# The causal mask of an attention moved from TensorE's product into VectorE's row maximum

## What is computed

```
H, DH, RAMP, NEG = 16, 64, 32, -1000000000.0
q, k, v = heads of query @ Wq, query @ Wk, query @ Wv        # 8 x 16 heads x 1024 x 64
w = jnp.einsum('bhqd,bhkd->bhqk', q, k) / DH
causal = jnp.triu(jnp.full((s, s), NEG, dtype=w.dtype), k=1)
w = jax.nn.softmax(w + causal, axis=-1)
mask = jnp.clip((arange(s) + span_val * s) / (RAMP + 1), 0.0, 1.0)   # per head, per key
w = w * mask
w = w / (jnp.sum(w, axis=-1, keepdims=True) + 1e-08)
out = (w @ v, heads side by side) @ Wo
```

## Time and profile before

| | |
|---|---|
| runs | median 3530.09 us of 3 (3526.44 to 3532.24) |
| profiled execution | span 3527.3 us; no separate time beside it, so the median lies 2.8 us above this span |
| TensorE busy in the span | 3383.0 us (96%) |
| VectorE | 2916.8 us (83%) |
| ScalarE | 2350.8 us (67%) |
| GpSimd | 848.4 us (24%) |
| mask products L1360 | 1024, from 581.4 to 3009.1 us |
| row maxima L1542 | 1024, 766.1 us busy |

### The profile page before, as it was taken

How to read it: one execution, slowest core, us unless ns; L and a number is a source line. 1 busy time by engine, 2 the same in 40 slices (tenths; PEclk the granted TensorE clock), 3 DMA queues, 4 the chain that set the end, 5 groups by cost and what they waited for, 6 DMA issues and landing times.

```text
span 3527.3 us, 77883 instructions
## 1 busy us (share of the span) xinstructions
PE 3383.0 (96%) x29872; PEld 3071.4 (87%) x29872; DVE 2916.8 (83%) x4672; ACT 2350.8 (67%) x4307; POOL 848.4 (24%) x911
## 2 busy tenths in 40 slices
PE   4999996999999999999999999999999999799998
PEld 4999995888888888888888888888888888699998
DVE  8999974888888888888888878878887888899996
ACT  4666543677777777777767777777777777465664
POOL 3443321221222122122122122212122212233332
PEclk9999997999999999999999999999999999899999
DMA  3332204345445455455445445545534545111111
GB/s 123 95 123 87 93 33 124 97 117 125 125 109 126 109 142 125 112 125 122 109 126 137 116 109 134 125 103 141 134 98 107 145 104 153 54 49 55 55 54 37
DMA packets 160338, 375.19 MB, mean 106 GB/s; under 512 B 19824, under 2 KB 62832, under 8 KB 159728
## 3 DMA queue, kind: packets, MB, share of 16 engines
q1 hardware_dynamic: 159984, 370.37, 40.0%
HBM read 129.38 MB, written 39.58 MB: 48 GB/s over the span
## 4 chain that ended last, share of the span: by engine, by line
PE 64%; DVE 10%; issue 6%; ACT 2%; POOL 2%; POOLq 0%; ACTq 0%; DVEq 0%
PE at_t_ps L1370 11%; PE at_side_ps L1285 9%; PE at_o_ps L1386 8%; PE ffn_gu_ps L505 7%; PE at_s_ps L1356 6%; PE at_s_ps L1357 6%; PE at_side_ps L1297 5%; PE at_side_ps L1334 4%; PE ffn_down_ps L530 4%; DVE at_neg_max L1542 3%; DVE at_eT_lo L1548 3%; PE at_s_ps L1360 1%; PE ffn_hT_ps L475 1%; PE at_side_ps L1324 1%; DVE at_oT_lo L1510 1%
## 5 line engine op out<-in xcount | busy, mean ns | idle before, releaser
L1548 DVE SCALAR_TENSOR_TENSOR at_eT_lo<-at_t_ps,at_eT_hi 128x512 f16<-128x512 f32 (+3 forms) x1536 | 852.2, 555 | 328.8 <-ACT at_eT_hi L1462 322.9
L1462 ACT ACTIVATE at_eT_hi<-at_t_ps 128x512 f16<-128x512 f32 (+3 forms) x1536 | 756.7, 493 | 333.3 <-PE at_t_ps L1370 322.6
L1455 ACT ACTIVATE at_e_rows<-at_s_ps,at_neg_max 128x1024 f32<-128x1024 f32 (+7 forms) x1024 | 759.7, 742 | 152.2 <-DVE at_neg_max L1542 144.7
L1370 PE MATMUL at_t_ps<-at_ident,at_e_rows 128*128 128x128 f32 x4608 | 798.8, 284 | 0.0
L1542 DVE TENSOR_REDUCE at_neg_max<-at_s_ps 128x1 f32<-128x1024 f32 (+7 forms) x1024 | 766.1, 748 | 19.4 <-PE at_s_ps L1360 15.6
L1386 PE MATMUL at_o_ps<-at_v_cols,at_eT_hi 128*128 128x132 f16 x4608 | 611.5, 222 | 2.1 <-DVE at_eT_lo L1548 1.6
L1356 PE MATMUL at_s_ps<-at_kh_st,at_q_st 128*128 128x512 f32 (+2 forms) x1536 | 583.0, 380 | 19.0 <-issue 9.1
L1386 PE MATMUL at_o_ps<-at_v_cols,at_eT_lo 128*128 128x66 f16 x4608 | 567.2, 192 | 0.0
L1357 PE MATMUL at_s_ps<-at_kl_st,at_q_st 128*128 128x512 f32 (+2 forms) x1536 | 514.1, 342 | 0.0
L1370 PEld LDWEIGHTS at_t_ps<-at_ident,at_e_rows 128*128 128x128 f32 x4608 | 491.7, 141 | 0.1
L1386 PEld LDWEIGHTS at_o_ps<-at_v_cols,at_eT_hi 128*128 128x128 f16 x4608 | 432.5, 98 | 25.7 <-issue 18.8
(11 more groups left out here) (211 smaller groups left out, 7088.3 us busy)
## 6 DMA issues: line engine op xcount, KB each, us to landing
at_kh_st<-at_k_hi SPq DMA_DIRECT2D x256, 256.0 KB, 4.5
at_kl_st<-at_k_lo SPq DMA_DIRECT2D x256, 256.0 KB, 5.9
at_w_qk<-w_qk_split SPq DMA_DIRECT2D x65, 512.0 KB, 7.4
at_q_st<-at_q_hi SPq DMA_DIRECT2D x128, 256.0 KB, 3.8
at_q_st<-at_q_lo SPq DMA_DIRECT2D x128, 256.0 KB, 4.8
at_w_v<-w_v_split SPq DMA_DIRECT2D x66, 256.0 KB, 6.0
at_w_out<-w_out_split SPq DMA_DIRECT2D x32, 512.0 KB, 3.7
ffn_x_rows<-in_L_attn_query_dram SPq DMA_DIRECT2D x32, 256.0 KB, 3.2
```

The costliest lines, as they stand in the source:

```text
L1370: last = nc.tensor.transpose(t_ps[i % TBUF][:, b * P:(b + 1) * P], e_rows[:, n % 4, (k0 + b) * P:(k0 + b + 1) * P], ident[:])
L1455: nc.scalar.activation(e_rows[:, n % 4, :w], s_ps[n % 2][:, col:col + w], ACT.Exp, bias=neg_max[:, n % 4:n % 4 + 1]).then_inc(sem("exp_don ...
L1462: nc.scalar.activation(eT[0][:, i % EBUF, :count * P], t_ps[i % TBUF][:, :count * P], ACT.Copy, scale=PSCALE).then_inc(sem("eT_hi"), 1)
L1548: nc.vector.scalar_tensor_tensor(out=eT[1][:, i % EBUF, :count * P], in0=t_ps[i % TBUF][:, :count * P], scalar=PSCALE, in1=eT[0][:, i % EB ...
```

## The change

The mask product is left out. `strip` is a row of 1024 numbers per partition in SBUF: zeros, and in its last 128 columns the triangle with +1e9 above the diagonal. Queries are now scaled by -1/64 rather than 1/64, so the score buffer holds negated scores. `row_max` becomes a fused VectorE instruction that reads the negated scores from PSUM and the last w columns of the strip from SBUF, writes their sum into `e_rows` in SBUF, and reduces it to a minimum. The exponential then runs from `e_rows` to `e_rows`, with scale -1. The wait for a free buffer of `e_rows` (`turned`) moves from ScalarE to VectorE, and the score product waits for `max_done` of the unit two before it, no longer for `exp_done`.

```diff
@@ GpSimd, at the start
-            for name, t in (("ident", ident), ("ident_b", ident_b)):
+            for t in (ident, strip):
                 nc.gpsimd.memset(t[:], 0.0).then_inc(sem("zeroed"), 1)
-            nc.gpsimd.memset(causal[:], 0.0).then_inc(sem("zeroed"), 1)
...
-            nc.gpsimd.affine_select(out=causal[:], in_=causal[:], compare_op=ALU.is_ge, fill=NEG, base=0,
+            nc.gpsimd.affine_select(out=strip[:, SEQ - P:], in_=strip[:, SEQ - P:], compare_op=ALU.is_ge, fill=-NEG, base=0,
                                     pattern=[[-1, P]], channel_multiplier=1)
@@ TensorE, scores
-                pe.wait_ge(sem("exp_done"), g * NU + (n - 1 + AHEAD["exp_done"]))
+                pe.wait_ge(sem("max_done"), g * NU + (n - 1 + AHEAD["max_done"]))
...
-                    if lastc:
-                        diag = col + j * P - k0
-                        last = nc.tensor.matmul(s_ps[n % 2][:, diag:diag + P], ident_b[:], causal[:], start=False, stop=True)
@@ ScalarE, exp
-                act.wait_ge(sem("max_done"), g * NU + (n + 1))
-                act.wait_ge(sem("turned"), g * NG + (LAST_GROUP[(n - 4) % NU] + 1 + (n - 4) // NU * NG + AHEAD["turned"]))
-                nc.scalar.activation(e_rows[:, n % 4, :w], s_ps[n % 2][:, col:col + w], ACT.Exp, bias=neg_max[:, n % 4:n % 4 + 1])
+                act.wait_ge(sem("max_done"), g * NU + (n + 1 + AHEAD["max_done"]))
+                nc.scalar.activation(e_rows[:, n % 4, :w], e_rows[:, n % 4, :w], ACT.Exp, bias=neg_max[:, n % 4:n % 4 + 1],
+                                     scale=-1.0)
@@ VectorE, row_max
+                w = P * (j + 1)
                 dve.wait_ge(sem("scores_done"), g * NU + (n + 1))
-                nc.vector.tensor_reduce(neg_max[:, n % 4:n % 4 + 1], s_ps[n % 2][:, col:col + P * (j + 1)], AX.X, ALU.max,
-                                        negate=True)
+                dve.wait_ge(sem("turned"), g * NG + (LAST_GROUP[(n - 4) % NU] + 1 + (n - 4) // NU * NG + AHEAD["turned"]))
+                nc.vector.tensor_tensor_reduce(e_rows[:, n % 4, :w], s_ps[n % 2][:, col:col + w], strip[:, SEQ - w:], 1.0, BIGGEST,
+                                               ALU.add, ALU.min, neg_max[:, n % 4:n % 4 + 1])
```

More of the change, by code:

```diff
@@ L571 @@
 SUM_EPS = 1e-8
+BIGGEST = 3.0e38
 PSCALE = 2.0 ** 14
@@ L1092, in attention @@
         oT = [sb(f"oT_{part}", [P, 2, QT, P], F32R) for part in ("hi", "lo")]
-        ident, ident_b, causal = sb("ident", [P, P]), sb("ident_b", [P, P], BF16), sb("causal", [P, P], BF16)
+        ident = sb("ident", [P, P])
+        strip = sb("strip", [P, SEQ])
         s_ps = [pb("s_ps0", [P, 2 * CHUNK]), pb("s_ps1", [P, CHUNK])]
@@ L1194, in _ @@
         def _(pool):
[L1195 removed]
+            for t in (ident, strip):
                 nc.gpsimd.memset(t[:], 0.0).then_inc(sem("zeroed"), 1)
[L1197 to L1203 removed]
+            pool.wait_ge(sem("zeroed"), 2)
+            nc.gpsimd.affine_select(out=ident[:], in_=ident[:], compare_op=ALU.not_equal, fill=1.0, base=0,
                                     pattern=[[-1, P]], channel_multiplier=1).then_inc(sem("consts"), 1)
+            nc.gpsimd.affine_select(out=strip[:, SEQ - P:], in_=strip[:, SEQ - P:], compare_op=ALU.is_ge, fill=-NEG, base=0,
+                                    pattern=[[-1, P]], channel_multiplier=1).then_inc(sem("masked"), 1)
             for vc in v_cols:
@@ L1356, in scores @@
                     nc.tensor.matmul(out, qs, kh_st[par][a][:, k0:k0 + w], start=True, stop=False)
-                    last = nc.tensor.matmul(out, qs, kl_st[par][a][:, k0:k0 + w], start=False, stop=not lastc)
-                    if lastc:
-                        diag = col + j * P - k0
-                        last = nc.tensor.matmul(s_ps[n % 2][:, diag:diag + P], ident_b[:], causal[:], start=False, stop=True)
+                    last = nc.tensor.matmul(out, qs, kl_st[par][a][:, k0:k0 + w], start=False, stop=True)
                 last.then_inc(sem("scores_done"), 1)
@@ L1394, in start @@
                         pe.wait_ge(sem("xT_lo"), 4)
-                    out.append(piece(kind, c, 0, 0, 0, 1, out[n - 4] if n >= 4 else ("consts", 3), start_ps[n % 4]))
+                    out.append(piece(kind, c, 0, 0, 0, 1, out[n - 4] if n >= 4 else ("consts", 1), start_ps[n % 4]))
                 scores(0, 0, 0)
@@ L1439, in piece @@
                 if kind in ("q", "k"):
-                    copy_side(side[kind][0][:, cols], f"{kind}_done", 2 * g + (c + 1), f"{kind}_hi", 1.0 / DH if kind == "q" else 1.0, bank)
+                    copy_side(side[kind][0][:, cols], f"{kind}_done", 2 * g + (c + 1), f"{kind}_hi", -1.0 / DH if kind == "q" else 1.0, bank)
                 elif kind == "o_turn":
@@ L1448, in exp @@
             def exp(n, g, par):
-                a, j = UNITS[n]
-                col = score_chunks(j)[0][0]
-                w = P * (j + 1)
-                act.wait_ge(sem("max_done"), g * NU + (n + 1))
-                act.wait_ge(sem("turned"), g * NG + (LAST_GROUP[(n - 4) % NU] + 1 + (n - 4) // NU * NG + AHEAD["turned"]))
-                nc.scalar.activation(e_rows[:, n % 4, :w], s_ps[n % 2][:, col:col + w], ACT.Exp, bias=neg_max[:, n % 4:n % 4 + 1]).then_inc(sem("exp_done"), 1)
+                w = P * (UNITS[n][1] + 1)
+                act.wait_ge(sem("max_done"), g * NU + (n + 1 + AHEAD["max_done"]))
+                nc.scalar.activation(e_rows[:, n % 4, :w], e_rows[:, n % 4, :w], ACT.Exp, bias=neg_max[:, n % 4:n % 4 + 1],
+                                     scale=-1.0).then_inc(sem("exp_done"), 1)
             def turn_hi(i, g):
@@ L1617, in _ @@
             nc.vector.memset(power[:], -0.5).then_inc(sem("power"), 1)
-            for name in ("eT_lo", "wo_added"):
+            dve.wait_ge(sem("masked"), 1)
+            for name in ("eT_lo", "wo_added", "max_done"):
                 dve.sem_inc(sem(name), AHEAD[name])
```

12 lines of the change are left out of this document (4 added, 8 removed).

## The result

The changed kernel takes 3493.8 us (median of 4 runs, 3492.4 to 3497.8), the kernel before 3529.8 us beside it (3526.4 to 3532.2): a ratio of 0.9899, 95% interval 0.9885 to 0.9913, or 36.0 us less. The forecast's sum was -36 us.

The account below looks back on a forecast made before the run. The prediction took TensorE as the bound, with 4.9 us of each 37.6 us pair set by ScalarE and VectorE. Its sum, -55 + 15 - 2 + 6 = -36 us, gave 3494 us; 8-in-10 range 3465 to 3526.

Parts of the forecast that it names:

- Masks: Mask products removed from TensorE: 0.07 us each, 0.865 us on the chain per pair, 64 pairs, -55 us.
- late side pieces: Side pieces on TensorE now drained just in time come late: 0.1 us a pair, +6 us, between 0 and 9.
- share on the chain: Part of a pair's 16 masks on the chain of waits: 13 and 11 in two pairs, mean 0.865 us.
- VectorE's maxima: Fused maximum plus second instruction 0.12 us dearer each, two of a pair's 16 on the path: +15 us.
- ScalarE's exponential: Exponential reading SBUF, not PSUM: some 0.03 us longer each, 32 us in all, hidden by ScalarE's idle time: 0.
- The scores' wait: Scores on TensorE wait for the maximum, no longer the exponential: -2 us, between nothing and 4.9.
- GpSimd's constants: GpSimd fills 1024 columns ahead of the identity the first transposition needs: 0, within 1 us either way, once.
- The signs: Forecast wrong if: 1024-column fused instruction over 1.6 us, its partner over 0.3, or new at_eT_lo waits in every pair.
- VectorE as the bound: Rival: fused instruction takes more than one cycle per element; at half rate +271 us, 3801 us; 15 in 100.
- Full gain: Rival: second VectorE instruction overlaps and mid-pair waits shrink; 3453 us at best, 3474 with half; 15 in 100.
- The gain eaten: Rival: VectorE's second instruction pays full latency, TensorE stands longer at side pieces; no change, 3534 us; 10 in 100.

Follow-up runs that it names:

- E1: The kernel before without its mask product, the causal mask left out of the computation; 3488.1 us, ratio 0.9882.
- E11: The kernel before with the mask product issued twice; 3577.2 us, ratio 1.0131.
- E6: The changed kernel with the exponential reading PSUM and scores waiting for it again, the mask in the maximum alone; 3496.6 us, ratio 0.9905.
- E5: The kernel before with the fused maximum over a strip of zeros, the mask product staying on TensorE, the exponential reading PSUM; 3531.2 us, ratio 1.0006.
- E10: The changed kernel with a 128x64 copy from PSUM to SBUF on VectorE ahead of each fused maximum; 3548.2 us, ratio 1.0051.
- E3: The changed kernel with scores waiting again for the exponential of the unit two before, nothing else undone; 3500.4 us, ratio 0.9922.
- E2: The kernel before with the fused maximum over zeros and the exponential reading SBUF, masks and scores' wait as before; 3533.9 us, ratio 1.0010.

## Why the prediction was right, and which of its terms were not

**Masks, -55, and late side pieces, +6: measured together -40.4 (E1), -38.2 in the attention.** The share on the chain, 12.4 of 16, holds (12.1 to 12.5 in E11). The price of 0.07 us was too high, in two ways. A second mask behind the first costs 0.06 (E11). And the rows for one mask were read without their successor. From the start of the last key product to the second value product it is 1630.14 to 1630.50 before, and 1612.62 to 1612.93 after, in the timelines of TensorE of both kernels:

```profile
1630.50 0.19 PE L1386 MATMUL at_o_ps<-at_v_cols,at_eT_lo 128*128 128x66 f16 x1
```

```profile
1612.62 0.40 PE L1357 MATMUL at_s_ps<-at_kl_st,at_q_st 128*128 128x512 f32 x1
1612.86 0.23 PE L1383 MATMUL at_o_ps<-at_v_cols,at_eT_hi 128*128 128x132 f16 x1
1612.93 0.19 PE L1383 MATMUL at_o_ps<-at_v_cols,at_eT_lo 128*128 128x66 f16 x1
```

0.36 against 0.31 us: the mask is worth 0.05 us net at this place, since the value product behind it now has the dearer start that the mask had (0.24 from the key product, 0.07 to the next). 0.01 us of rounding is 8 us in the product, so the mean over all units decides: 0.291 us before, 0.235 in E1, 0.056 net. At 12.4 masks a pair that is 64 x 12.4 x 0.056 = 44 us. What E1 lacks of it is 4 us by the medians and 6 by the stretch, and that is what is left for late pieces; the forecast had 6. So the price is the term that was mis-sized, 44 for 55. The late pieces are a remainder and were not measured by themselves: the waits shown for side pieces grew by 23 us (30.2 - 7.6), more than the remainder. Waits that the modelled ends had hidden may have come into view; this isn't shown.

**VectorE's maxima, +15: measured +8.5 with the masks off (E6 - E1), of which 3.5 in the attention, and +2.7 with them on (E5).** This is the step that failed, twice over. "I take 0.115 us, with the 5 ns 0.12 us for each maximum" was wrong: the read overlaps the fused instruction's tail, and start to start shows less than 0.01. The argument that it must wait for the result that it reads did not hold. "The other 14 of a pair are covered by VectorE's idle time" was wrong as well: E10 shows 6.5 of 16 on the path. With the measured price it is 64 x 6.5 x 0.009 = 4 us, about the 3.5 of the stretch. At 0.12 us each, by the same share, 64 x 6.5 x 0.12 = 50 us would have come back (an estimate from E10), and the change would have gained nothing. A price far too high and a share far too low offset one another in part; that is luck. The Trainium skill (Vector Engine (DVE) Microarchitecture Reference, section 5.2) gives some 75 ns per instruction after overlap: the profile shows 83 ns as the read's duration, but its price on VectorE is 0.01 us or less here, so the measurement decides. Its section 7, on half throughput for one shape of instruction with two non-bf16 sources in SBUF, did not strike, as its words said: 1216 ns at 1024 columns with one source in PSUM.

**ScalarE's exponential, 0: measured +3.7 (E3 - E6) and +2.8 (E2 - E5); in the attention's stretch +6.1 and +2.3.** The 33 ns hold; "nothing" does not. 33 ns are 34 us for 1024, of which between a fifteenth and a fifth is on the path.

**The scores' wait, -2: measured -6.6.** At the first scores the forecast holds: from the first score product to the one of the third unit it is 4.64 us in E3 and 3.47 in the changed kernel, 1.17 us less, where 1.1 had been forecast. The other 5 us are not located. Scores waited 6.1 us for an exponential in E3 and wait 1.3 for a maximum in the changed kernel, but there value products wait 3.4 us for `at_o_raw`, which E3's list doesn't have.

**GpSimd's constants, 0.** GpSimd starts on them at 549.89 us (550.28 before), and the first transposition starts at 552.44 (551.82 before): 2.55 us behind against 1.54, so 1.0 us later, at the edge of the bound. The mechanism is another than the one forecast: the identity's select is over at 551.42, as before or sooner. VectorE now waits for the strip (its select ends at 551.67) ahead of the first semaphores that it gives, and the row of this transposition names VectorE's queue (L1580) as what it waited for. Neither this nor the move of `turned` to VectorE was tried alone; E5 has the wait for `turned` on VectorE as well, beside the fused instruction, and its stretch of the attention is 0.6 us longer.

**The signs.** None of the three that would have shown the forecast wrong came: 1216 ns at 1024 columns, 83 ns for its partner, and 2.1 us in two waits for `at_eT_lo`. They were too wide to catch what was wrong. The three numbers that did were those of VectorE's next start, of its busy share and of the pair's middle, and all three missed.

**The rivals.** VectorE as the bound: excluded by the full rate of the fused instruction. Full gain: its first half, that the second instruction overlaps, is what happened. Its price is excluded by E1, which has nothing of VectorE's part and still returns only 40 us of the 72. The gain eaten: it did not happen, but E10 shows how near it was. By that share a second instruction of 0.12 us would have been enough, without the exponentials that I thought it needed.

The ladder in one line: -40.4 + 8.5 + 3.7 - 6.6 = -34.8, and -36.0 by the medians of the first comparison; the forecast's -49 + 15 + 0 - 2 = -36. In the attention's stretch it is -38.2 + 3.5 + 6.1 - 6.6 = -35.1, with rounding: VectorE's part is 11.5 us below its forecast and the wait 5 below, the masks are 11 and the exponential 6 above.

No version tried beats the changed kernel with the same result: E1, at 3488.1, leaves the mask out. The 6 us to it are not all that the form of the mask costs, since E1 still has the old wait: by the ladder the fused instruction and the exponential's source cost 10 to 12 us together.

## What to carry to other kernels

Price a second instruction by the starts around it, not by its duration, and price a removed one by the distance between the neighbours that stay. The chain of one execution names the instructions that are late now, not those that would be late after 0.1 us more: here 2 of 16 maxima stood on it, and 6.5 of 16 counted as soon as something was added, so the share read off the chain was three times too small, though idle time per unit seemed to cover the rest. And when two medians differ by a few microseconds, look in the traces whether the difference lies in the part that was changed: of the 8.5 us between E6 and E1 less than half did. Before an instruction is moved, list everything that waits for it and everything queued behind it on each engine; the move of one maximum by one group cost 121 us, most of what the waits show of it through a score buffer and a copy that had nothing to do with it.
